# Router logits of a fused attention and mixture-of-experts kernel as half-precision products of high and low parts

## Chip, cores and metric

One Trainium2 chip, one core. The metric is the device time of one execution in microseconds (us); shown times are medians of several executions of the same program.

## What is computed

Two blocks with residuals over 4096 rows of 256 numbers. In the first, every row has its own small attention: the row is cut into 16 heads of 16, and heads attend to heads of the same row.

```python
x = x + xattn(layernorm(x), ctx, ctx)         # per row: 16x16 scores, causal, softmax, times values
xf = layernorm(x).reshape(-1, 256)
logits = xf @ gate_w.T + gate_b               # 8 experts
top1 = argmax(logits)                         # one expert a row
for e in range(8):
    y = relu(xf @ w1[e].T + b1[e]) @ w2[e].T + b2[e]
    out = out + where(top1 == e, y, 0)
x = x + out
```

The kernel takes the logits of the rows before the layer norm: they are `rstd * (x1 @ gate_w.T) + shift * sum(gate_w) + gate_b`, so the product with `gate_w` needs only x1, the outputs of the first block.

## The kernel before

Names in capitals are engines: TensorE (PE), VectorE (DVE), ScalarE (ACT), GpSimd (POOL), SyncE (SP, which only starts DMAs).

**Stage one** runs over 16 chunks of 256 rows, in 4 groups of 4 chunks. Per chunk PE makes scores (`s_ps`, 96 half-precision products, L1403), DVE takes row maxima and subtracts, ACT exponentiates (L849), DVE sums and inverts (`inverse`, L1000), POOL multiplies by the inverse (`a_sb`, L1304), PE turns the weights (`at_ps`, L1420), ACT and DVE split them into a high and a low half-precision part, and PE multiplies by the values (`pv_ps`, L1433). Queries, keys and values are split in the same way: ACT writes the high part (L786, L794, L802), POOL subtracts it from the original and writes the low part (L1282, L1289, L1296). Queries and values are then copied by DMA into block diagonals (`spread`, L601), issued by SP and ACT. DVE adds the residual and leaves x1 of the chunk in `o_sb` (L1012), 128 partitions x 32 rows x 16 heads in single precision.

**Per group**, when its 4 chunks stand in `o_sb`, PE does 4 steps of turned outputs (`tr_ps`, L1445, four transposes each) and 4 steps of gates (`lg_ps`, L1459, four heads each). ACT copies each turned step into `pay` (L842), and the next step waits for that copy (`s_x1`). From `pay` DVE takes layer-norm statistics; from the logits it chooses the expert and the slot of each row, and POOL scatters the group's 1024 rows to `sorted_rows` in DRAM by 8 indirect DMAs (L1340). The first copy of the next group into `pay` waits until these have landed (`s_scatter`).

**Stage two** runs over 39 tiles of 128 rows of one expert each: up (L1506), split of the hidden values, down (L1522, L1523), result to DRAM by an indirect DMA (L1366). It starts while the last group's logits and turned outputs are still to be done; these are woven between its first matrix products.

**The order** on each engine is written out by hand: the table `TIMES` has a number for each step of each lane, and `weave` issues the steps of an engine by these numbers. Each engine runs its instructions in that order, and a wait on one holds up all that stand behind it. A gate step is

```python
for h in range(4 * n, 4 * n + 4):
    m = eng.matmul(LG, o_sb[:, :, h], gate_bd[:, h].rearrange("p b e -> p (b e)"), start=h == 0, stop=h == HEADS - 1)
```

in which `gate_bd` (L915, made once by DVE, 128x1024) holds the gate weights in diagonal blocks. The product is in single precision; the trace has two records for each.

Of the kernel before, what the change touches and what calls it, by code (L numbers as in the profile page):

```python
# [8 lines left out]
F16 = mybir.dt.float16  # L9
# [3 lines left out]
ALU = mybir.AluOpType  # L13
# [3 lines left out]
P = 128  # L17
HEADS = 16
# [5 lines left out]
G = 8  # L24
# [51 lines left out]
    },  # L76
    "ACT": {
        "weights": (
# [136 lines left out]
    },  # L215
    "POOL": {
        "constants": (85, 155, 283),
        "tables": (399,),
# [137 lines left out]
def xattn_moe_kernel(nc, x, x_t, x_r, k_t, v_t, gate_w, gate_b, w1, b1, w2, b2, out):  # L356
# [26 lines left out]
    with stack:  # L383
# [18 lines left out]
        region = sb("region", [P, E])  # L402
        gate_bd = sb("gate_bd", [P, HEADS, 8, E])
        owner = sb("owner", [P, 8])
# [31 lines left out]
        inverse = sb("inverse", [P, BLK])  # L436
        o_sb = sb("o_sb", [P, P, HD])

        pay = sb("pay", [P, G, ROW])
# [38 lines left out]
        def carve(flat, cols):  # L478
# [52 lines left out]
        s_o_t, s_x1, s_bn, s_var1, s_rstd1, s_ln1, s_logits, s_eighths, s_gate_cols, s_gate_sum, s_gate_bd = [sem(n) for n in  # L531
            ("s_o_t", "s_x1", "s_bn", "s_var1", "s_rstd1", "s_ln1", "s_logits", "s_eighths", "s_gate_cols", "s_gate_sum", "s_gate_bd")]
        s_hot, s_seen, s_ranked, s_slot, s_tail = [sem(n) for n in ("s_hot", "s_seen", "s_ranked", "s_slot", "s_tail")]
        s_plan, s_planned, s_packed, s_digit, s_lists, s_count, s_filler = [sem(n) for n in
# [77 lines left out]
        def _(eng):  # L612
# [31 lines left out]
            def load_residual():  # L644
                for i in range(NC):
                    yield
                    sp.wait_ge(s_o_t, 4 * (i // CG))
                    sp.wait_ge(s_logits, i // CG)
                    eng.dma_start(o_sb[:, i % CG * BLK:(i % CG + 1) * BLK, :], xr_v[:, i]).then_inc(s_xr[i % CG], 16)
# [127 lines left out]
        def _(eng):  # L777
# [57 lines left out]
            def turned_rows():  # L835
                for g in range(NG):
                    for n in range(4):
# [41 lines left out]
            def relus():  # L879
                for j in range(NTILES):  # L880
# [6 lines left out]

            weave(TIMES["ACT"], spread_first_queries=spread_first_queries(), spread=spread(), queries=queries(),
                  keys=keys(), values=values(), turned_rows=turned_rows(), exponentials=exponentials(),
                  weights=weights(), expert_inputs=expert_inputs(), relus=relus())  # L890

        @block.vector
        def _(eng):
            dve = Line(eng)

            def constants():
# [15 lines left out]
                yield  # L912
                dve.wait_ge(s_select, 3)
                dve.wait_ge(s_gate, 32)
                eng.tensor_tensor(gate_bd[:], gate_sb.rearrange("p (h e) -> p h e", e=E).unsqueeze(2)  # L915
                                  .to_broadcast([P, HEADS, 8, E]), owner[:].unsqueeze(1).unsqueeze(3)
                                  .to_broadcast([P, HEADS, 8, E]), ALU.mult).then_inc(s_gate_bd, 1)
                yield
# [60 lines left out]
            def softmax():  # L979
                a = a_sb[:].rearrange("p (n k) -> p n k", k=HEADS)  # L980
                for i in range(NC):
                    yield
                    dve.wait_ge(s_qk, i + 1)
                    dve.wait_ge(s_minus_max, i)
                    eng.tensor_reduce(rowmax[:], s_ps[i % 2], AX_X, ALU.max).then_inc(s_max, 1)
                    yield
                    dve.wait_ge(s_max, i + 1)
                    dve.wait_ge(s_turned, i)
                    dve.wait_ge(s_gate_bd, 1)
# [43 lines left out]
            def choose():  # L1033
# [3 lines left out]
                for g in range(NG):  # L1037
# [9 lines left out]
                    dve.wait_ge(s_logits, g + 1)  # L1047
                    eng.tensor_tensor(v[0], lg, pay[:, :, D + 1:D + 2].to_broadcast([P, G, E]), ALU.mult).then_inc(s_hot, 1)
                    yield
# [188 lines left out]
        def _(eng):  # L1238
# [60 lines left out]
            def weights_of_softmax():  # L1299
                a = a_sb[:].rearrange("p (n k) -> p n k", k=HEADS)  # L1300
                for i in range(NC):
# [3 lines left out]
                                      ALU.mult).then_inc(s_a, 1)  # L1305

            def tables():
                yield
# [52 lines left out]
            def stores():  # L1361
                for j in range(NTILES):
# [9 lines left out]
            weave(TIMES["POOL"], constants=constants(), zeros=zeros(), statistics=statistics(), queries=queries(), keys=keys(),  # L1372
                  values=values(), weights_of_softmax=weights_of_softmax(), tables=tables(),
                  layer_norms=layer_norms(), row_tails=row_tails(), scatters=scatters(),
                  skipped_rows=skipped_rows(), residuals=residuals(), stores=stores())

        @block.tensor
        def _(eng):
# [69 lines left out]
            def gates():  # L1448
                for g in range(NG):
                    for n in range(4):  # L1450
                        yield
                        if n == 0:
                            pe.wait_ge(s_gate_bd, 1)
                            pe.wait_ge(s_o, CG * (g + 1))
                            pe.wait_ge(s_slot, 4 * g - 3)
                            if g > STAGES[0][2]:
                                pe.wait_ge(s_plan, PLAN * (g - STAGES[0][2] - 1) + 1)
                        for h in range(4 * n, 4 * n + 4):
                            m = eng.matmul(LG, o_sb[:, :, h], gate_bd[:, h].rearrange("p b e -> p (b e)"), start=h == 0,  # L1459
                                           stop=h == HEADS - 1)  # L1460
                    m.then_inc(s_logits, 1)
# [99 lines left out]
```

## Time and profile before

| | |
|---|---|
| median of 3 executions | 464.17 us (463.13 to 464.6) |
| profiled execution | span 462.9 us from its first to its last instruction; the page has no other time of it |
| busy | PE 83%, DVE 73%, ACT 39%, POOL 45% |
| chain that ended last | PE 58%, DVE 12%, issue 8%, SP's queue 7%, POOL 6%, DMA 5%, ACT 2% |

Stage one ends about 230 us into the span, stage two fills the rest. The chain follows the work that ended last back to what released it, step by step; an engine's share in it is what a faster engine could give at most. Idle times in the timeline stand in brackets behind an instruction, with what ended them.

### The profile page before, as it was taken

The page shows a single profiled execution, that of the slowest core. Times are in us where ns is not written, and L with a number is a line of the kernel's source. Part 1 is how long each engine was busy: PE and PEld are TensorE (multiplying, and loading weights), DVE is VectorE, ACT ScalarE, POOL GpSimd, SP SyncE. Part 2 cuts the span into 40 slices and gives each one's busy share as a digit, 9 for nine tenths or more (in the row PEclk, how much of TensorE's full clock was granted, in tenths as well). Part 3 has the DMA queues.
Part 4 walks back from the last instruction along what each step waited for, and adds up shares of the span by engine and source line. Part 5 has one row for each costly group of instructions (what it writes and reads, how often), then busy time and mean ns, then how long its engine had stood idle before and what let it go on. Part 6 is the DMA issues. An engine that isn't in the chain of part 4 may idle for free.

```text
span 462.9 us, 16301 instructions
## 1 busy us (share of the span) xinstructions
PE 384.6 (83%) x5889; PEld 328.5 (71%) x5889; DVE 339.8 (73%) x777; ACT 181.1 (39%) x317; POOL 207.6 (45%) x213
## 2 busy tenths in 40 slices
PE   0126878996798969895699999898999999999991
PEld 0026767996698869894688877676788888787870
DVE  8789799789882875378676987596867677766761
ACT  2344446454542523143353433243443434434320
POOL 8536444635673548643342354743333233233321
PEclk9999999955555555565589999999999999999998
DMA  7999989889778675667552544757543443434310
GB/s 264 417 254 236 264 220 260 260 188 240 200 161 218 159 160 112 180 141 219 125 143 67 107 98 106 186 139 184 106 94 99 95 108 90 104 84 106 100 29 0
DMA packets 125802, 73.17 MB, mean 158 GB/s; under 512 B 99229, under 2 KB 110238, under 8 KB 125216
## 3 DMA queue, kind: packets, MB, share of 16 engines
q1 hardware_dynamic: 96336, 60.46, 50.6%
q0 software_dynamic: 3408, 8.46, 5.0%
q10 hardware_dynamic: 25984, 3.21, 4.9%
q8 instruction: 52, 0.85, 0.7%
q14 instruction: 22, 0.18, 0.1%
HBM read 48.28 MB, written 11.24 MB: 129 GB/s over the span
## 4 chain that ended last, share of the span: by engine, by line
PE 58%; DVE 12%; issue 8%; SPq 7%; POOL 6%; DMA 5%; ACT 2%; POOLq 0%; DVEq 0%; ACTq 0%
PE s_ps L1506 19%; PE at_ps L1522 7%; PE pv_ps L1522 6%; PE s_ps L1403 6%; PE pv_ps L1433 5%; PE lg_ps L1459 4%; DMA arena<-qv_hl 3%; PE at_ps L1523 3%; PE pv_ps L1523 3%; SPq L601 3%; PE tr_ps L1445 2%; DVE arena L1186 2%; PE at_ps L1420 2%; POOL sorted_rows L1340 1%; POOL qv_hl L1296 1%
## 5 line engine op out<-in xcount | busy, mean ns | idle before, releaser
L1506 PEld LDWEIGHTS s_ps<-arena 128*128 x1872 | 131.9, 99 | 43.4 <-issue 4.9
L1506 PE MATMUL s_ps<-arena 128*128 128x128 f16 x1872 | 157.0, 221 | 2.8 <-issue 1.2
L1203 DVE SCALAR_TENSOR_TENSOR arena<-arena,s_ps 128x512 f32<-128x512 f32 x78 | 53.5, 685 | 32.5 <-PE s_ps L1506 21.1
L1433 PE MATMUL pv_ps<-a_hl,arena 128*128 128x16 f16 x1536 | 54.6, 180 | 17.1 <-DMA arena<-qv_hl 12.3
L1433 PEld LDWEIGHTS pv_ps<-a_hl,arena 128*128 128x128 f16 x1536 | 53.3, 118 | 20.7 <-DMA arena<-qv_hl 16.7
L1366 POOL DMA_INDIRECT result<-arena x39 | 38.9, 996 | 64.4 <-DVE arena L1228 60.3
L1403 PEld LDWEIGHTS s_ps<-k_hl,arena 128*128 128x128 f16 x1536 | 54.5, 118 | 15.4 <-DMA arena<-qv_hl 10.6
L1522 PE MATMUL at_ps<-arena,k_in 128*128 x160 | 60.3, 379 | 2.8 <-DVE k_hl L1214 2.8
L1359 POOL TENSOR_TENSOR arena<-arena 128x256 f32<-128x256 f32 x39 | 29.5, 756 | 73.4 <-DMA arena<-b 73.3
L1403 PE MATMUL s_ps<-k_hl,arena 128*128 128x16 f16 x1536 | 54.2, 180 | 9.7 <-DMA arena<-qv_hl 9.7
L1522 PE MATMUL pv_ps<-arena,x_in 128*128 x152 | 57.6, 379 | 0.0
L886 ACT ACTIVATE k_in<-arena 128x512 f16<-128x512 f32 x40 | 25.2, 629 | 60.5 <-DVE arena L1203 49.2
L1186 DVE SCALAR_TENSOR_TENSOR arena<-arena 128x512 f16<-128x512 f32 x56 | 47.7, 871 | 1.1 <-ACT arena L863 1.1
L863 ACT ACTIVATE arena<-arena 128x512 f16<-128x512 f32 x56 | 33.5, 623 | 33.3 <-issue 12.1
L886 ACT ACTIVATE x_in<-arena 128x512 f16<-128x512 f32 x38 | 23.9, 630 | 56.5 <-DVE arena L1203 42.0
L1523 PE MATMUL at_ps<-arena,k_hl 128*128 x160 | 43.6, 272 | 0.3 <-issue 0.3
L1523 PE MATMUL pv_ps<-arena,x_in 128*128 x152 | 41.4, 272 | 0.0
L1340 POOL DMA_INDIRECT sorted_rows<-pay,slot_i x32 | 33.2, 1037 | 15.2 <-issue 7.7
L1214 DVE SCALAR_TENSOR_TENSOR k_hl<-arena,k_in 128x512 f16<-128x512 f32 x40 | 27.4, 686 | 13.4 <-ACT k_in L886 13.0
L1282 POOL TENSOR_TENSOR qv_hl<-x_in,qv_hl 128x512 f16<-128x512 f32 x16 | 22.1, 1383 | 33.6 <-ACT qv_hl L786 33.6
L1214 DVE SCALAR_TENSOR_TENSOR x_in<-arena,x_in 128x512 f16<-128x512 f32 x38 | 27.0, 710 | 10.2 <-ACT x_in L886 9.4
L1459 PE MATMUL lg_ps<-gate_bd,o_sb 128*128 128x64 f32 x128 | 29.8, 408 | 2.3 <-DVE o_sb L1012 2.3
(141 smaller groups left out, 589.9 us busy)
## 6 DMA issues: line engine op xcount, KB each, us to landing
arena<-w SPq DMA_DIRECT2D x28, 512.0 KB, 5.1
arena<-sorted_rows SPq DMA_DIRECT2D x39, 130.0 KB, 2.2
arena<-b SPq DMA_DIRECT2D x39, 128.0 KB
arena<-qv_hl SPq DMA_DIRECT2D x70, 64.0 KB
k_in<-k_t SPq DMA_DIRECT2D x16, 256.0 KB
arena<-x SPq DMA_DIRECT2D x4, 1024.0 KB, 10.6
x_in<-x_t SPq DMA_DIRECT2D x16, 256.0 KB, 5.0
v_in<-v_t SPq DMA_DIRECT2D x16, 256.0 KB
```

Source lines behind the costliest of these rows:

```text
L886: eng.activation(h_hi[j % 2][:, c * HALF:(c + 1) * HALF], h_in[:, c], ACT.Relu).then_inc(s_h_hi, 1)
L1186: eng.scalar_tensor_tensor(out=lo, in0=src, scalar=W_SCALE, in1=hi, op0=ALU.mult, op1=ALU.subtract).then_inc(s_w_lo, 1)
L1203: eng.scalar_tensor_tensor(out=h_in[:, c].rearrange("p (k t) -> p k t", t=P), in0=bias, scalar=W_SCALE, in1=h_ps[c][:].rearrange("p (k t) ...
L1214: eng.scalar_tensor_tensor(out=h_lo[j % 2][:, cols], in0=h_in[:, c], scalar=0.0, in1=h_hi[j % 2][:, cols], op0=ALU.max, op1=ALU.subtract). ...
L1340: eng.indirect_dma_start(out=sorted_rows, out_offset=bass.IndirectOffsetOnAxis(ap=slot_i[:, b:b + 1], axis=0), in_=pay[:, b, :], in_offset ...
L1366: eng.indirect_dma_start(out=out, out_offset=bass.IndirectOffsetOnAxis(ap=rows[:, r, :].bitcast(I32)[:, D + 2:D + 3], axis=0), in_=rows[:, ...
L1403: m = eng.matmul(s[:, n], q_bd[i % 2][:, n // 2, :, n % 2, q], k_hl[:, n, k, :], start=False, stop=(n, q) == (BLK - 1, 1))
L1433: m = eng.matmul(o[:, n], v_bd[i][:, n // 2, :, n % 2, v], a_hl[:, n, a, :], start=(n, a, v) == (0, 0, 0), stop=(n, v) == (BLK - 1, 1))
L1459: m = eng.matmul(LG, o_sb[:, :, h], gate_bd[:, h].rearrange("p b e -> p (b e)"), start=h == 0, stop=h == HEADS - 1)
L1506: k = eng.matmul(o, weights_of(j, w + k_ * H + n * P, P), xt[:, j % XB, a + k_], start=(k_, w, a) == (0, HI_1, 0), stop=k_ == KD - 1 and w ...
L1522: eng.matmul(y[:], h_hi[j % 2][:, n * P:(n + 1) * P], weights_of(j, at, 2 * D), start=n == 0, stop=False)
L1523: k = eng.matmul(y[:, 0:D], h_lo[j % 2][:, n * P:(n + 1) * P], weights_of(j, at, D), start=False, stop=n == KH - 1)
```

## The change

1. DVE no longer makes `gate_bd`. It makes `gate_hl`, the gate weights times 64 in a high and a low half-precision part (two instructions of 128x128), and POOL makes the block diagonals of both parts (two instructions of 128x1024, lane `gate_blocks`).
2. For each of the 16 chunks ACT writes the high part of the chunk of `o_sb` into `o_hl`, and POOL the low part (lanes `output_halves`). `o_hl` is laid out partition, head, row, part: the elements that one of these instructions writes one after the other lie 512 bytes apart.
3. A gate step is 12 half-precision products of 128x64 in place of 4 in single precision: high by high, high by low, low by high, for each head. It waits for the high and low parts of all 4 chunks (`s_o_hi`, `s_o_lo`), where it waited for `s_o`.
4. DVE divides by 64 in the instruction that multiplies the logits by `rstd`.
5. SP's reload of `o_sb` waits for the split of the chunk that stood there, in place of the logits of its group. ACT's split of a group's first chunk waits for the logits of the group before.
6. The buffer in SBUF for descriptors of POOL's DMAs is set to 2048 bytes a partition; it had its default size.

All other numbers of `TIMES` stay.

```diff
+        "output_halves": (5316, 6999, 7544, 7821, 10139, 11102, 11887, 12396, 14641, ...    # ACT
+        "gate_blocks": (2900,),                                                            # POOL
+        "output_halves": (5386, 7069, 7614, 7891, 10209, 11172, 11957, 12466, 14711, ...   # POOL
-        gate_bd = sb("gate_bd", [P, HEADS, 8, E])
+        gate_bd = sb("gate_bd", [P, HEADS, 2, 8, E], F16)
+        gate_hl = sb("gate_hl", [P, 2, HEADS * E], F16)
+        o_hl = sb("o_hl", [P, HEADS, P, 2], F16)
...
                     sp.wait_ge(s_o_t, 4 * (i // CG))
-                    sp.wait_ge(s_logits, i // CG)
+                    sp.wait_ge(s_o_hi, i - CG + 1)
+                    sp.wait_ge(s_o_lo, i - CG + 1)
...
+            def output_halves():                                                           # ACT
+                for i in range(NC):
+                    at = slice(i % CG * BLK, (i % CG + 1) * BLK)
+                    yield
+                    act.wait_ge(s_o, i + 1)
+                    act.wait_ge(s_logits, i // CG)
+                    eng.copy(o_hl[:, :, at, 0].rearrange("p h t -> p t h"), o_sb[:, at, :]).then_inc(s_o_hi, 1)
...
-                eng.tensor_tensor(gate_bd[:], gate_sb.rearrange(...), owner[:]..., ALU.mult).then_inc(s_gate_bd, 1)
+                eng.tensor_scalar(gate_hl[:, 0], gate_sb, W_SCALE, None, ALU.mult).then_inc(s_gate_hl, 1)
+                dve.wait_ge(s_gate_hl, 1)
+                eng.scalar_tensor_tensor(out=gate_hl[:, 1], in0=gate_sb, scalar=W_SCALE, in1=gate_hl[:, 0], op0=ALU.mult,
+                                         op1=ALU.subtract).then_inc(s_gate_hl, 1)
...
+            def gate_blocks():                                                             # POOL
+                yield
+                pool.wait_ge(s_select, 3)
+                pool.wait_ge(s_gate_hl, 2)
+                for n in range(2):
+                    eng.tensor_tensor(gate_bd[:, :, n], gate_hl[:, n]..., owner[:]..., ALU.mult).then_inc(s_gate_bd, 1)
+
+            def output_halves():                                                           # POOL
+                for i in range(NC):
+                    at = slice(i % CG * BLK, (i % CG + 1) * BLK)
+                    hi, lo = [o_hl[:, :, at, n].rearrange("p h t -> p t h") for n in range(2)]
+                    yield
+                    pool.wait_ge(s_o_hi, i + 1)
+                    eng.tensor_tensor(lo, o_sb[:, at, :], hi, ALU.subtract).then_inc(s_o_lo, 1)
...
-                            pe.wait_ge(s_gate_bd, 1)
-                            pe.wait_ge(s_o, CG * (g + 1))
+                            pe.wait_ge(s_gate_bd, 2)
+                            pe.wait_ge(s_o_hi, CG * (g + 1))
+                            pe.wait_ge(s_o_lo, CG * (g + 1))
...
                         for h in range(4 * n, 4 * n + 4):
-                            m = eng.matmul(LG, o_sb[:, :, h], gate_bd[:, h]..., start=h == 0, stop=h == HEADS - 1)
+                            for a, w in ((0, 0), (0, 1), (1, 0)):
+                                m = eng.matmul(LG, o_hl[:, h, :, a], gate_bd[:, h, w]..., ...)
...
-    nc = bacc.Bacc("TRN2", target_bir_lowering=False, num_devices=1)
+    nc = bacc.Bacc("TRN2", target_bir_lowering=False, num_devices=1, dynamic_dma_scratch_size=2048)
```

Where the new instructions stand on POOL is seen in its order. In the changed kernel L1322 is the multiplication by the inverse, L1300, L1307 and L1314 are the low parts of queries, keys and values, L1375 is a scatter, L1340 the new low part of the outputs; before they were L1304, L1282, L1289, L1296 and L1340.

**POOL, around the scatters of the first group** (the chunks whose outputs are split here are those of the second group). Before:

```order
L1296 TENSOR_TENSOR qv_hl<-v_in,qv_hl 128x512
L1304 TENSOR_TENSOR a_sb<-a_sb,inverse 128x512
L1282 TENSOR_TENSOR qv_hl<-x_in,qv_hl 128x512
L1340 DMA sorted_rows<-pay,slot_i 35840x260 x3
L1289 TENSOR_TENSOR k_hl<-k_in,k_hl 128x32x16
L1340 DMA sorted_rows<-pay,slot_i 35840x260
L1296 TENSOR_TENSOR qv_hl<-v_in,qv_hl 128x512
L1304 TENSOR_TENSOR a_sb<-a_sb,inverse 128x512
L1282 TENSOR_TENSOR qv_hl<-x_in,qv_hl 128x512
L1340 DMA sorted_rows<-pay,slot_i 35840x260 x4
```

Now:

```order
L1314 TENSOR_TENSOR qv_hl<-v_in,qv_hl 128x512 [waits s_v_hi]
L1340 TENSOR_TENSOR o_hl<-o_sb,o_hl 128x32x16 [waits s_o_hi]
L1322 TENSOR_TENSOR a_sb<-a_sb,inverse 128x512 [waits s_inverse]
L1300 TENSOR_TENSOR qv_hl<-x_in,qv_hl 128x512 [waits s_q_hi]
L1375 DMA sorted_rows<-pay,slot_i 35840x260 [waits s_ln1,s_x1,s_tail,s_slot]
L1375 DMA sorted_rows<-pay,slot_i 35840x260 x2
L1307 TENSOR_TENSOR k_hl<-k_in,k_hl 128x32x16 [waits s_k_hi]
L1375 DMA sorted_rows<-pay,slot_i 35840x260
L1340 TENSOR_TENSOR o_hl<-o_sb,o_hl 128x32x16 [waits s_o_hi]
L1314 TENSOR_TENSOR qv_hl<-v_in,qv_hl 128x512 [waits s_v_hi]
L1322 TENSOR_TENSOR a_sb<-a_sb,inverse 128x512 [waits s_inverse]
L1300 TENSOR_TENSOR qv_hl<-x_in,qv_hl 128x512 [waits s_q_hi]
```

One low part stands ahead of the multiplication by the inverse, one between the fourth and the last four scatters, and a third follows the last row shown, ahead of these four.

**POOL, at the scatters of the second group.** Before:

```order
L1304 TENSOR_TENSOR a_sb<-a_sb,inverse 128x512
L1340 DMA sorted_rows<-pay,slot_i 35840x260
L1282 TENSOR_TENSOR qv_hl<-x_in,qv_hl 128x512
L1340 DMA sorted_rows<-pay,slot_i 35840x260 x3
L1289 TENSOR_TENSOR k_hl<-k_in,k_hl 128x32x16
```

Now:

```order
L1322 TENSOR_TENSOR a_sb<-a_sb,inverse 128x512 [waits s_inverse]
L1375 DMA sorted_rows<-pay,slot_i 35840x260
L1340 TENSOR_TENSOR o_hl<-o_sb,o_hl 128x32x16 [waits s_o_hi]
L1300 TENSOR_TENSOR qv_hl<-x_in,qv_hl 128x512 [waits s_q_hi]
L1340 TENSOR_TENSOR o_hl<-o_sb,o_hl 128x32x16 [waits s_o_hi]
L1375 DMA sorted_rows<-pay,slot_i 35840x260 x3
L1307 TENSOR_TENSOR k_hl<-k_in,k_hl 128x32x16 [waits s_k_hi]
```

Two low parts stand ahead of the last six scatters; the second of them is what the third group's first gate step waits for.

**POOL, at the scatters of the third group**, where stage two begins. Before:

```order
L1304 TENSOR_TENSOR a_sb<-a_sb,inverse 128x512
L1340 DMA sorted_rows<-pay,slot_i 35840x260 x6
L1359 TENSOR_TENSOR arena<-arena 128x256
L1340 DMA sorted_rows<-pay,slot_i 35840x260 x2
L1359 TENSOR_TENSOR arena<-arena 128x256 x2
```

Now:

```order
L1375 DMA sorted_rows<-pay,slot_i 35840x260
L1340 TENSOR_TENSOR o_hl<-o_sb,o_hl 128x32x16 [waits s_o_hi]
L1375 DMA sorted_rows<-pay,slot_i 35840x260
L1340 TENSOR_TENSOR o_hl<-o_sb,o_hl 128x32x16 [waits s_o_hi]
L1375 DMA sorted_rows<-pay,slot_i 35840x260 x3
L1394 TENSOR_TENSOR arena<-arena 128x256 [waits s_b2_0,s_xn2]
L1375 DMA sorted_rows<-pay,slot_i 35840x260 x2
```

Here too two low parts stand ahead of six of the eight scatters, and the last group's gates wait for the second.

## Rows read from the trace of the kernel before

**Rows 1.** The page: the span, and the chain that ended last by line.

```profile
span 462.9 us, 16301 instructions
...
PE s_ps L1506 19%; PE at_ps L1522 7%; PE pv_ps L1522 6%; PE s_ps L1403 6%; PE pv_ps L1433 5%; PE lg_ps L1459 4%; DMA arena<-qv_hl 3%; PE at_ps L1523 3%; PE pv_ps L1523 3%; SPq L601 3%; PE tr_ps L1445 2%; DVE arena L1186 2%; PE at_ps L1420 2%; POOL sorted_rows L1340 1%; POOL qv_hl L1296 1%
```

**Rows 2.** The chain in order of time: start, duration, what.

```profile
82.40 1.61 PE lg_ps L1459 x8
...
138.29 4.58 DMA sorted_rows<-pay,slot_i
142.97 0.59 ACT pay L842
143.61 1.12 PE tr_ps L1445 x4
```

**Rows 3.** Groups by shape: busy, mean ns, idle before; one row of ACT's timeline.

```profile
L1282 POOL TENSOR_TENSOR qv_hl<-x_in,qv_hl 128x512 f16<-128x512 f32 x16 | 22.1, 1383 | 33.6 <-ACT qv_hl L786 33.6
L1289 POOL TENSOR_TENSOR k_hl<-k_in,k_hl 128x512 f16<-128x512 f32 x16 | 20.1, 1255 | 10.9 <-ACT k_hl L794 10.8
...
116.69 0.79 ACT L786 CAST qv_hl<-x_in 128x512 f16<-128x512 f32 x1 [0.56 <-DVE x_in L977]
```

**Rows 4.** Timeline of PE, half-precision products: start, duration, instruction, count.

```profile
108.14 3.36 PE L1403 MATMUL s_ps<-k_hl,arena 128*128 128x16 f16 x96
111.39 0.39 PE L1468 MATMUL lg_ps<-onehot,ones_bf 128*128 128x56 bf16 x7
```

**Rows 5.** Timeline of POOL and PE, end of the first group's gates.

```profile
91.52 1.06 POOL L1304 TENSOR_TENSOR a_sb<-a_sb,inverse 128x512 f32<-128x512 f32 x1 [1.41 <-DVE inverse L1000]
...
93.49 1.06 PE L1420 MATMUL at_ps<-ident,a_sb 128*128 128x128 f32 x4
```

**Rows 6.** Timeline of POOL, second group.

```profile
119.05 1.06 POOL L1304 TENSOR_TENSOR a_sb<-a_sb,inverse 128x512 f32<-128x512 f32 x1 [3.71 <-DVE inverse L1000]
120.07 1.79 POOL L1282 TENSOR_TENSOR qv_hl<-x_in,qv_hl 128x512 f16<-128x512 f32 x1
...
132.70 1.28 POOL L1282 TENSOR_TENSOR qv_hl<-x_in,qv_hl 128x512 f16<-128x512 f32 x1 [1.80 <-ACT qv_hl L786]
...
167.61 1.06 POOL L1304 TENSOR_TENSOR a_sb<-a_sb,inverse 128x512 f32<-128x512 f32 x1 [1.34 <-DVE inverse L1000]
```

**Rows 7.** Timeline of POOL, PE and ACT, third group.

```profile
181.23 1.01 POOL L1340 DMA_INDIRECT sorted_rows<-pay,slot_i  x1 [0.17 <-issue]
...
181.78 1.97 PE L1459 MATMUL lg_ps<-gate_bd,o_sb 128*128 128x64 f32 x8
...
191.21 0.97 POOL L1340 DMA_INDIRECT sorted_rows<-pay,slot_i  x1 [0.30 <-issue]
...
196.72 0.59 ACT L842 COPY pay<-tr_ps 128x512 f32<-128x512 f32 x1 [0.49 <-issue]
...
197.53 1.09 PE L1445 MATMUL tr_ps<-ident,o_sb 128*128 128x128 f32 x4
```

**Rows 8.** Timeline of PE, POOL and ACT, last group and start of stage two.

```profile
227.91 2.00 PE L1459 MATMUL lg_ps<-gate_bd,o_sb 128*128 128x64 f32 x8 [1.71 <-DVE o_sb L1012]
...
228.54 0.97 POOL L1340 DMA_INDIRECT sorted_rows<-pay,slot_i  x1 [0.30 <-issue]
...
239.11 0.59 ACT L842 COPY pay<-tr_ps 128x512 f32<-128x512 f32 x1 [1.93 <-DMA sorted_rows<-pay,slot_i]
...
239.97 0.60 PE L1445 MATMUL tr_ps<-ident,o_sb 128*128 128x128 f32 x4
```

**Rows 9.** Timeline of DVE and POOL, the first 60 us.

```profile
20.56 1.39 DVE L915 TENSOR_TENSOR gate_bd<-a_sb,owner 128x1024 f32<-128x1024 f32 x1
...
32.04 1.27 POOL L1282 TENSOR_TENSOR qv_hl<-x_in,qv_hl 128x512 f16<-128x512 f32 x1 [4.40 <-ACT qv_hl L786]
...
52.51 0.69 DVE L1012 TENSOR_TENSOR o_sb<-pv_ps,o_sb 128x512 f32<-128x512 f32 x1
...
54.95 1.30 POOL L1296 TENSOR_TENSOR qv_hl<-v_in,qv_hl 128x512 f16<-128x512 f32 x1 [1.31 <-ACT qv_hl L802]
```

More of the change, by code:

```diff
@@ L77 @@
     "ACT": {
+        "output_halves": (5316, 6999, 7544, 7821, 10139, 11102, 11887, 12396, 14641, 15353, 16633, 16750, 19138, 19643, 20641, 20747),
         "weights": (
@@ L216 @@
     "POOL": {
+        "gate_blocks": (2900,),
+        "output_halves": (5386, 7069, 7614, 7891, 10209, 11172, 11957, 12466, 14711, 15423, 16703, 16820, 19208, 19713, 20711, 20817),
         "constants": (85, 155, 283),
@@ L532, in xattn_moe_kernel @@
             ("s_o_t", "s_x1", "s_bn", "s_var1", "s_rstd1", "s_ln1", "s_logits", "s_eighths", "s_gate_cols", "s_gate_sum", "s_gate_bd")]
+        s_gate_hl, s_o_hi, s_o_lo = [sem(n) for n in ("s_gate_hl", "s_o_hi", "s_o_lo")]
         s_hot, s_seen, s_ranked, s_slot, s_tail = [sem(n) for n in ("s_hot", "s_seen", "s_ranked", "s_slot", "s_tail")]
@@ L888, in _ @@
             weave(TIMES["ACT"], spread_first_queries=spread_first_queries(), spread=spread(), queries=queries(),
-                  keys=keys(), values=values(), turned_rows=turned_rows(), exponentials=exponentials(),
+                  keys=keys(), values=values(), turned_rows=turned_rows(), output_halves=output_halves(),
+                  exponentials=exponentials(),
                   weights=weights(), expert_inputs=expert_inputs(), relus=relus())
@@ L912, in constants @@
                 yield
-                dve.wait_ge(s_select, 3)
                 dve.wait_ge(s_gate, 32)
-                eng.tensor_tensor(gate_bd[:], gate_sb.rearrange("p (h e) -> p h e", e=E).unsqueeze(2)
-                                  .to_broadcast([P, HEADS, 8, E]), owner[:].unsqueeze(1).unsqueeze(3)
-                                  .to_broadcast([P, HEADS, 8, E]), ALU.mult).then_inc(s_gate_bd, 1)
+                eng.tensor_scalar(gate_hl[:, 0], gate_sb, W_SCALE, None, ALU.mult).then_inc(s_gate_hl, 1)
+                dve.wait_ge(s_gate_hl, 1)
+                eng.scalar_tensor_tensor(out=gate_hl[:, 1], in0=gate_sb, scalar=W_SCALE, in1=gate_hl[:, 0], op0=ALU.mult,
+                                         op1=ALU.subtract).then_inc(s_gate_hl, 1)
                 yield
@@ L988, in softmax @@
                     dve.wait_ge(s_turned, i)
-                    dve.wait_ge(s_gate_bd, 1)
+                    dve.wait_ge(s_gate_hl, 2)
                     dve.wait_ge(s_gate_cols, 1)
@@ L1047, in choose @@
                     dve.wait_ge(s_logits, g + 1)
-                    eng.tensor_tensor(v[0], lg, pay[:, :, D + 1:D + 2].to_broadcast([P, G, E]), ALU.mult).then_inc(s_hot, 1)
+                    eng.scalar_tensor_tensor(out=v[0], in0=lg, scalar=1.0 / W_SCALE,
+                                             in1=pay[:, :, D + 1:D + 2].to_broadcast([P, G, E]), op0=ALU.mult,
+                                             op1=ALU.mult).then_inc(s_hot, 1)
                     yield
@@ L1305, in weights_of_softmax @@
                                       ALU.mult).then_inc(s_a, 1)
+            def gate_blocks():
[3 more added lines that the diff above has]
+                for n in range(2):
+                    eng.tensor_tensor(gate_bd[:, :, n], gate_hl[:, n].rearrange("p (h e) -> p h e", e=E).unsqueeze(2)
+                                      .to_broadcast([P, HEADS, 8, E]), owner[:].unsqueeze(1).unsqueeze(3)
+                                      .to_broadcast([P, HEADS, 8, E]), ALU.mult).then_inc(s_gate_bd, 1)
+            def output_halves():
[5 more added lines that the diff above has]
+                    eng.tensor_tensor(lo, o_sb[:, at, :], hi, ALU.subtract).then_inc(s_o_lo, 1)
             def tables():
@@ L1373, in _ @@
                   values=values(), weights_of_softmax=weights_of_softmax(), tables=tables(),
+                  gate_blocks=gate_blocks(), output_halves=output_halves(),
                   layer_norms=layer_norms(), row_tails=row_tails(), scatters=scatters(),
@@ L1458, in gates @@
                         for h in range(4 * n, 4 * n + 4):
-                            m = eng.matmul(LG, o_sb[:, :, h], gate_bd[:, h].rearrange("p b e -> p (b e)"), start=h == 0,
-                                           stop=h == HEADS - 1)
+                            for a, w in ((0, 0), (0, 1), (1, 0)):
+                                m = eng.matmul(LG, o_hl[:, h, :, a], gate_bd[:, h, w].rearrange("p b e -> p (b e)"),
+                                               start=(h, a, w) == (0, 0, 0), stop=(h, a) == (HEADS - 1, 1))
                     m.then_inc(s_logits, 1)
```

## The prediction

> **What bounds the kernel now.** I read the page first, then the chain by line, then the chain in order of time, then the timelines of PE, POOL, ACT and DVE around the four places where logits are made, and last the groups by shape for prices. The reader should see three things. First, the gate products (L1459) are 4% of the chain of 462.9 us [rows 1], some 18 us; one step of four heads takes 1.61 us [rows 2], and there are 16 steps. So a shorter gate step can give time back, but not more than this. Second, the chain does not stay on PE in stage one. Between the first and the second group it runs through POOL: the last scatter of the first group at 138.29, its landing, ACT's copy into the same buffer at 142.97, and PE's transposes at 143.61, which had nothing else to wait for [rows 2]. What delays a scatter there delays everything. Third, POOL, though idle half of the time, is idle in stage one because it waits in order for one operand after the other; new work in its order is free only where it falls into such a wait.
>
> All sums are made against the profiled execution, span 462.9 us [rows 1]; the median of the three executions, 464.17, is 1.3 us above it, and I add the differences to the median. About 0.3% (1.4 us) is what a measurement here can tell from no change.
>
> **Prices of the new pieces.** (a) A gate step of 12 products of 128x64. The nearest rows are 96 products with 16 columns in 3.36 us, 35 ns each, and 7 with 56 down to 8 columns in 0.39 us, 56 ns each [rows 4]; the first bounds from below (0.42 us a step), 128-column weights being loaded in both; I take the second, 0.65 us, since it has nearly as many columns. So a step loses 1.0 us, and 16 steps lose 16 us of PE. (b) ACT's high part: 0.79 us, as the cast of queries at 116.69 [rows 3], which also writes 2 bytes at a time with gaps [rows 3]. (c) POOL's low part, T. The subtraction for keys, packed in runs of 16 elements, takes 1.26 us, that for queries, every second element, 1.38, and the slowest of the latter 1.79 [rows 3, 6]. The new one writes and reads each element 512 bytes from the last one, so it stands nearer to the queries; I take T = 1.38, with 1.26 and 1.79 as ends. No row here shows a step this wide.
>
> **The sum, place by place.**
>
> *First 60 us.* DVE's L915, 1.39 us [rows 9], becomes two instructions of 128x128, by size about 0.55 us together: 0.8 less on DVE, which is on the chain there. POOL gets two of 128x1024; twice L1304's 1.06 [rows 5] makes 2.1 each, 4.2 together, and POOL's idle time before 32.04 is 4.40 [rows 9]: just hidden. The first chunk's low part can start after L1012 ends at 53.20 and the cast, at 54.0, and ends at 55.4, where POOL's next step began at 54.95 [rows 9]: 0.45 late. I count half of the 0.8 as gained, since loads that must land stand behind it: together 0, ends -0.8 and +1.5.
>
> *First group.* Here the low parts fit in POOL's waits, and PE is on the chain from the first gate step past 93.49. Four shorter steps would give 4.0, but each transposes step waits for ACT's copy of the one before, and the transposes at 93.49 need POOL's 91.52 to 92.58 [rows 5], itself behind DVE work that moves by about half a microsecond; they come 1.4 earlier, the last gate step gives 1.2 more, and DVE takes 0.3 back: -2.3, ends 0 and -4.0.
>
> *Second group.* POOL now has a low part ahead of L1304 at 119.05 (its high part can come right behind ACT's cast at 116.69 [rows 3], at 117.48 to 118.27, so it ends at 119.65: 0.6 late), one ahead of the last four scatters (T), and one more right behind L1282 at 132.70 (T, and 0.1 for ACT). The 1.80 idle before 132.70 [rows 6] absorbs nothing, for it was a wait on ACT, whose cast waits for POOL's values through its DMA issues; that moves along. So the last four scatters come 0.6 + 1.38 + 1.48 = 3.5 later, and PE's transposes at 143.61 with them. The three gate steps ahead of these lie in this wait, and PE's first one waits for the last low part; only the last step, behind, gives 1.0 back: +2.5. Then a low part ahead of L1304 at 167.61 [rows 6], with 1.34 idle before it of which half is usable: +0.5.
>
> *Third group.* Low part, queries, low part stand after the scatter at 181.23, so the first gate step, which began at 181.78 [rows 7], begins at 182.2 + 1.38 + 1.28 + 1.38 = 186.3. PE makes most of this up by shorter steps. The scatters make it up nowhere: the one at 191.21 goes 2.8 later. From scatter to copy took 4.7 in the first group (138.29 to 142.97 [rows 2]), so here it was ready at 195.9 and had 0.8 to spare before 196.72. The copy comes 2.0 later, the transposes at 197.53 [rows 7] 1.8, and the gate step behind them gives 1.0 back: +0.8.
>
> *Last group.* Two low parts stand between the scatters, one on each side of that at 228.54; the first gate step moves from 227.91 to 232 [rows 8], and stage two's first products behind it, which wait later for DVE anyway and are nearly level by 239. But the copy at 239.11 waited for the scatters, without slack [rows 8]; with 2.8 more it comes at 241.9, ACT's relus stand behind it, and the transposes at 239.97 start at 242.5: +2.5. The last gate step gives 1.2 back: +1.3. After that PE is full and nothing changes.
>
> Sum: 0 - 2.3 + 2.5 + 0.5 + 0.8 + 1.3 = **+2.8, so 467.0 us**. About nine times T lies on the path: T = 1.26 makes it +1.7, T = 1.79 +6.5.
>
> DVE's changed logits instruction keeps its size, and SP's looser wait on the reload of `o_sb` moves nothing: the low part it waits for belongs to the group before, done long since. ACT's DMAs of the block diagonals come up to 1.5 us later where a cast stands ahead of them; SP's issues of the same copies end at about that time, which covers it; without that cover the second group has 0.5 more.
>
> **The rivals.**
>
> *The wide step costs POOL more.* As slow as 1.79 each, the sum is +6.5, 470.7 us. For it: no subtraction in the trace has a step over 4 bytes, and the 4-byte one is already dearer than the packed one. Against it: that rise is only 0.13 [rows 3], and the 1.79 is one instance, probably disturbed by DVE. The Trainium skill, GPSIMD Engine Reference, section Performance pitfalls for Q7 kernels, says that a step of more than 8 bytes between elements read costs about half as much again per element; no run here shows that, and by it T would be 2.07 and the time 473, an estimate.
>
> *POOL's new work is hidden and PE's gain stays.* If the scatters were not what the next group waits for, or had slack, the four places would give -2.3, -1.0, -3.0 (three steps of the third group) and -1.3: 456.6 us, faster. For it: POOL is busy under half of the time, and the chain names L1459 with four times the share of the scatters [rows 1]. Against it: the transposes at 143.61 and the copies at 239.11 start when the scatters land [rows 2, 8]. It decides at whether the low parts between the scatters cost less than the gate steps behind them give.
>
> *Gain and loss cancel.* With T at 1.26 and half of the delay of the third group taken up, within 1.4 us of 464.2.
>
> *The products are not cheaper*, because weights with a step of two elements load slowly: at 0.13 us each a step takes 1.6, the gains of 2.3, 1.0, 1.0 and 1.2 fall away, 472.5 us. Scores already load weights with gaps at 35 ns each [rows 4], so this is unlikely. The smaller descriptor buffer could make POOL wait before a scatter; with 8 scatters a group landing within 5 us each, few are open at a time.
>
> **Chances.** The forecast, 465.6 to 469.5, has 0.37; the slow wide step 0.20; the last two 0.05; cancelling 0.18; hidden 0.20. Slower by over 0.3% is 0.62, within 0.18, faster 0.20. The range reaches from part of the way to the hidden case, 459.5, to beyond the dear products with a slow T, 474.
>
> **What would show it.** Right: a group of 16 POOL subtractions for `o_hl` near 1.4 us; gate steps near 0.65; the copy that stood at 142.97 about 1 us later, that at 239.11 some 5 us later; PE waiting for POOL at the first gate step of groups two to four. Wrong: gate steps over 1 us, low parts over 1.7 us, or the copies into `pay` no later than before, which would mean that POOL's order had room.

## The result, and the profile after

The change makes the kernel slower: 491.35 us median (490.28 to 491.73) beside 464.38 for the kernel before on the same chip, a ratio of 1.0565, 95% interval 1.0513 to 1.0617. That is 27 us more by the medians, 26 by the ratio, where 2.8 were forecast, and outside the range of 459.5 to 474.0. The profiled execution has a span of 489.4 us, 26.5 above that of before [rows 1]. The mean granted clock of TensorE is 0.845 in both, so nothing here points to the clock.

The page of the changed kernel, the span and the chain that ended last by line:

```profile
span 489.4 us, 16482 instructions
...
PE s_ps L1544 18%; PE at_ps L1560 6%; PE pv_ps L1560 6%; POOL o_hl L1340 4%; POOL sorted_rows L1375 4%; PE s_ps L1439 3%; ACT o_hl L858 3%; PE at_ps L1561 3%; PE pv_ps L1561 3%; DVE arena L1204 2%; POOL a_sb L1322 2%; DMA sorted_rows<-pay,slot_i 2%; POOL qv_hl L1300 2%; PE at_ps L1456 2%; POOL qv_hl L1314 2%
```

Of the gate products, 4% of the chain before [rows 1], five steps are left in it, 3.0 us together. In their place stand the two new steps: POOL's low parts (L1340) with 4% and ACT's high parts (L858) with 3%. The scatters (L1375) went from 1% to 4%. The prices are in the groups by line and shape (busy, mean ns, idle before):

```profile
L1340 POOL TENSOR_TENSOR o_hl<-o_sb,o_hl 128x512 f16<-128x512 f32 x16 | 41.2, 2576 | 26.3 <-ACT o_hl L858 26.2
L858 ACT CAST o_hl<-o_sb 128x512 f16<-128x512 f32 x16 | 39.8, 2521 | 10.5 <-DVE o_sb L1028 10.1 <-issue 0.4
L1497 PE MATMUL lg_ps<-gate_bd,o_hl 128*128 128x64 f16 x192 | 12.1, 234 | 28.2 <-issue 24.5 <-POOL o_hl L1340 3.6
L1330 POOL TENSOR_TENSOR gate_bd<-gate_hl,owner 128x1024 f16<-128x1024 f16 x2 | 3.8, 1928 | 0.0
```

A low part takes 2.58 us where I had 1.38, a cast 2.52 where I had 0.79. How the two enter the path can be read from the chain of the changed kernel in order of time (start, duration, what), third group:

```profile
185.31 0.58 DVE o_sb L1028
185.89 0.02 issue
185.91 2.48 ACT o_hl L858
188.40 0.07 issue
188.46 2.48 POOL o_hl L1340
190.94 0.77 POOL a_sb L1322
191.71 0.05 issue
191.75 0.47 PE at_ps L1456
```

An output is ready at 185.9; five microseconds later POOL is done with its halves, and only then comes the softmax weight (L1322), which PE's next transposes wait for and which has nothing to do with the halves except its place behind them in POOL's order.

The four copies into `pay` that answer to those of before (82.43 in the first group, and 142.97, 196.72 and 239.11 [rows 2, 7, 8]), timeline of ACT after:

```profile
91.91 0.57 ACT L849 COPY pay<-tr_ps 128x512 f32<-128x512 f32 x1
...
163.19 0.58 ACT L849 COPY pay<-tr_ps 128x512 f32<-128x512 f32 x1 [3.53 <-DMA sorted_rows<-pay,slot_i]
...
223.08 0.58 ACT L849 COPY pay<-tr_ps 128x512 f32<-128x512 f32 x1 [0.28 <-issue]
...
272.64 0.58 ACT L849 COPY pay<-tr_ps 128x512 f32<-128x512 f32 x1 [3.54 <-DMA sorted_rows<-pay,slot_i]
```

They come 9.5, 20.2, 26.4 and 33.5 us late. So the loss arises in stage one, some 6 to 11 us a group, and two of the copies, the second and the last, wait for scatters, as the sum had it. Stage two gives a little back (30.7 us late at DVE's result that stood at 445.81), and the last 4.2 come back behind the last store; that is an effect of its own, below.

A low part also delays work that does not stand behind it on POOL. One of DVE's splits of the expert weights (L1204, 0.68 us otherwise) begins while the low part at 179.24 runs, and ends 0.04 us after it; DVE's low part of the turned weights (L1019), on the way to the output above, follows at once:

```profile
179.24 3.01 POOL L1340 TENSOR_TENSOR o_hl<-o_sb,o_hl 128x512 f16<-128x512 f32 x1 [0.36 <-ACT o_hl L858]
...
179.83 2.46 DVE L1204 SCALAR_TENSOR_TENSOR arena<-arena 128x512 f16<-128x512 f32 x1
182.22 0.68 DVE L1019 TENSOR_TENSOR a_hl<-at_ps,a_hl 128x512 f16<-128x512 f32 x1
```

Two more, at 87.57 and 151.81, end in the same way within 0.06 us of a low part, after 2.28 and 2.14 us. The sum had no such wait.

### The profile page after: what moved, and what is told of

Same layout as the page of the kernel before. It is cut to its first block, busy times and chain, and to the rows that moved or that the text cites. A ratio compares the mean times of both kernels' runs of the same rounds, so it can differ in the third digit from the quotient of the medians.

```text
span 489.4 us, 16482 instructions
## 1 busy us (share of the span) xinstructions
PE 366.1 (75%) x5953; PEld 310.3 (63%) x5953; DVE 353.1 (72%) x778; ACT 218.3 (45%) x333; POOL 247.0 (50%) x231
## 4 chain that ended last, share of the span: by engine, by line
PE 44%; POOL 16%; DVE 11%; issue 10%; ACT 6%; DMA 6%; SPq 4%; ACTq 1%; POOLq 0%; DVEq 0%
PE s_ps L1544 18%; PE at_ps L1560 6%; PE pv_ps L1560 6%; POOL o_hl L1340 4%; POOL sorted_rows L1375 4%; PE s_ps L1439 3%; ACT o_hl L858 3%; PE at_ps L1561 3%; PE pv_ps L1561 3%; DVE arena L1204 2%; POOL a_sb L1322 2%; DMA sorted_rows<-pay,slot_i 2%; POOL qv_hl L1300 2%; PE at_ps L1456 2%; POOL qv_hl L1314 2%
## 5 line engine op out<-in xcount | busy, mean ns | idle before, releaser
L1469 PE MATMUL pv_ps<-a_hl,arena 128*128 128x16 f16 x1536 | 53.6, 180 | 19.2 <-DVE a_hl L1019 10.4
L1204 DVE SCALAR_TENSOR_TENSOR arena<-arena 128x512 f16<-128x512 f32 x56 | 53.5, 971 | 3.4 <-ACT arena L878 3.2
L1340 POOL TENSOR_TENSOR o_hl<-o_sb,o_hl 128x512 f16<-128x512 f32 x16 | 41.2, 2576 | 26.3 <-ACT o_hl L858 26.2
L878 ACT ACTIVATE arena<-arena 128x512 f16<-128x512 f32 x56 | 34.8, 645 | 32.9 <-issue 12.5
L858 ACT CAST o_hl<-o_sb 128x512 f16<-128x512 f32 x16 | 39.8, 2521 | 10.5 <-DVE o_sb L1028 10.1
L1456 PE MATMUL at_ps<-ident,a_sb 128*128 128x128 f32 x64 | 17.6, 431 | 31.9 <-POOL a_sb L1322 31.9
L1375 POOL DMA_INDIRECT sorted_rows<-pay,slot_i x32 | 32.7, 1022 | 13.8 <-issue 7.0
L1232 DVE SCALAR_TENSOR_TENSOR k_hl<-arena,k_in 128x512 f16<-128x512 f32 x40 | 27.9, 697 | 13.8 <-ACT k_in L901 13.7
```

Source lines behind the costliest of these rows:

```text
L858: eng.copy(o_hl[:, :, at, 0].rearrange("p h t -> p t h"), o_sb[:, at, :]).then_inc(s_o_hi, 1)
L1204: eng.scalar_tensor_tensor(out=lo, in0=src, scalar=W_SCALE, in1=hi, op0=ALU.mult, op1=ALU.subtract).then_inc(s_w_lo, 1)
L1340: eng.tensor_tensor(lo, o_sb[:, at, :], hi, ALU.subtract).then_inc(s_o_lo, 1)
L1375: eng.indirect_dma_start(out=sorted_rows, out_offset=bass.IndirectOffsetOnAxis(ap=slot_i[:, b:b + 1], axis=0), in_=pay[:, b, :], in_offset ...
L1469: m = eng.matmul(o[:, n], v_bd[i][:, n // 2, :, n % 2, v], a_hl[:, n, a, :], start=(n, a, v) == (0, 0, 0), stop=(n, v) == (BLK - 1, 1))
```

## The experiments

**Is it the step between the elements?** The high and low parts get tiles of their own, laid out like the outputs, so that they are written in runs ("packed"), in three versions (both, only the high part, only the low part):

```diff
-        o_hl = sb("o_hl", [P, HEADS, P, 2], F16)
+        o_hi = sb("o_hi", [P, P, HEADS], F16)
+        o_lo = sb("o_lo", [P, P, HEADS], F16)
```

> High and low parts go into two tiles laid out like the outputs, 16 heads side by side, so that ACT and POOL write (and POOL reads) runs of 2-byte elements, and TensorE's weights take every 16th element (32 bytes apart). Theory (price: the 512-byte step makes ACT's cast 2.52 us where I had 0.79 and POOL's subtraction 2.58 where I had 1.38, and these lie on the path): cast 0.6 to 0.8, subtraction 1.1 to 1.4, gate step still about 0.8, time 460 to 469, most of the 27 us back. Rival order (the place of the new steps in the two in-order queues costs the time, whatever they last): 478 or more. Rival weights (the 32-byte step moves the cost to TensorE): gate steps of 1.5 us or more, 470 to 480.

> Only the high part is packed; the low part keeps its 512-byte step. Theory price: ACT's cast 0.6 to 0.8; POOL reads packed and writes wide, and if the write is what costs it stays near 2.5, if the read is, it falls to 1.4. Time between the two others, 468 to 480: the casts' 1.7 us each come off the path, the subtractions' 1.2 stay. Rival (only POOL counts, ACT's casts are hidden): 485 or more.

> Only the low part is packed; the high part keeps its 512-byte step, so ACT writes wide (2.5 us) and POOL reads one operand wide and writes packed. Theory price: if the write costs, the subtraction falls to 1.2 to 1.5; if the read costs, it stays over 2. Time 472 to 484. Rival (only POOL counts): as packed.

Measured, as ratios to before: packed 1.0059 (1.0025 to 1.0092), only high packed 1.0337 (1.0297 to 1.0377), only low packed 1.0355 (1.0322 to 1.0388). With 464.66 for before that is 467.4, 480.3 and 481.2 us: the second lies just above the end of its range, the other two in theirs. The groups of POOL and ACT, first of the packed version, then with only the high part packed, then with only the low part packed:

```profile
L1341 POOL TENSOR_TENSOR o_lo<-o_sb,o_hi 128x512 f16<-128x512 f32 x16 | 19.6, 1222 | 7.4 <-ACT o_hi L859 7.3
...
L859 ACT CAST o_hi<-o_sb 128x512 f16<-128x512 f32 x16 | 9.8, 615 | 9.9 <-DVE o_sb L1029 9.5 <-issue 0.4
```

```profile
L1341 POOL TENSOR_TENSOR o_lo<-o_sb,o_hi 128x512 f16<-128x512 f32 x16 | 41.4, 2615 | 10.6 <-ACT o_hi L859 10.4
```

```profile
L859 ACT CAST o_hi<-o_sb 128x512 f16<-128x512 f32 x16 | 39.9, 2524 | 10.8 <-DVE o_sb L1029 10.5 <-issue 0.2
L1341 POOL TENSOR_TENSOR o_lo<-o_sb,o_hi 128x512 f16<-128x512 f32 x16 | 25.0, 1564 | 25.8 <-ACT o_hi L859 25.7
```

The layout takes 23.5 of the 26 us away (1.0565 less 1.0059, times 464.4). On POOL the wide **write** is the dear part: it doubles the step (2.62 against 1.22), while a wide read of one operand adds 0.34. The two halves share the loss. The wide write of the low part costs 0.0278 of 464.7, 12.9 us, for 1.39 more in each of 16 steps: it counts 9.3 times, and "about nine times T" had been the forecast. How much of this goes by POOL's order and how much by DVE's waits for POOL was not measured apart. The wide high part costs 13.8 us; less 9.3 times POOL's 0.34 for reading it, 10.6 are left for ACT's 1.91 more in each, which so counts 5.5 times, an estimate. The 12.9 and the 10.6 together are the 23.5 of the layout. The rivals fall: the order alone would have kept the time at 478 or more, and ACT's casts are not hidden when they last 2.5 us. TensorE pays little for weights with 32 bytes between elements: its loads take 165 ns on average where they took 126 in the changed kernel, a gate step some 0.9 us where it took some 0.8. First the packed version, then the changed kernel:

```profile
L1498 PEld LDWEIGHTS lg_ps<-gate_bd,o_hi 128*128 128x128 f16 x128 | 13.2, 165 | 16.5 <-issue 16.2
```

```profile
L1497 PEld LDWEIGHTS lg_ps<-gate_bd,o_hl 128*128 128x128 f16 x192 | 11.2, 126 | 29.1 <-issue 28.7
```

The differences between ratios carry some 2 us of uncertainty each.

**The price by itself.** A tail behind the last row of the changed kernel, one instruction at a time with nothing beside it:

```diff
+ladder(act, eng, "wr", lambda kind, step: eng.copy(stepped(step), like(wide_in, step)) if kind == "w"
+       else eng.copy(like(narrow[:], step), stepped(step)))
```

> The changed kernel with a tail after its last row, one instruction at a time: 512 elements of 128 partitions cast or subtracted with a step of 1, 2, 4, 8, 16, 32, 64, 128 and 256 elements (2 to 512 bytes) between the half-precision elements, twice each: ACT writes and reads with the step, DVE casts and subtracts with it, POOL writes, reads, and does both. Theory price: ACT's write goes from 0.6 to 0.8 at 2 and 4 bytes to 2.5 at 512, POOL's write from 1.2 to about 2.5, a rise somewhere between; reads cost less. Rival: all steps alike here, and the 2.5 us come from other traffic in the first stage (DMA or another engine at the same time).

The busy time of ACT's write in nine stretches (two instructions in each; the steps are 2, 4, 8, 16, 32, 64, 128, 256 and 512 bytes; shown are 2, 4, 8, 16 and 512):

```profile
core 0: us, ACT busy (x), PEclk, DMA share, GB/s
487.17:488.46 1.29, 1.24 (x2) 1.00 0.00 0
488.47:490.04 1.57, 1.52 (x2) 1.00 0.02 0
490.05:492.73 2.68, 2.63 (x2) 0.67 0.00 0
492.74:497.70 4.96, 4.91 (x2) 0.50 0.00 0
...
517.31:522.29 4.98, 4.93 (x2) 0.50 0.00 0
```

POOL's write at 4, 8, 16 and 512 bytes, and its read at 4, 8, 16 and 512 bytes, in the same view:

```profile
596.06:598.47 2.41, 2.31 (x2) 0.50 0.00 0
598.53:601.28 2.75, 2.65 (x2) 0.50 0.00 0
601.33:606.35 5.02, 4.91 (x2) 0.50 0.00 0
...
626.40:631.43 5.03, 4.93 (x2) 0.50 0.00 0
```

```profile
633.94:636.56 2.62, 2.52 (x2) 0.50 0.00 0
636.62:639.27 2.65, 2.55 (x2) 0.50 0.00 0
639.33:642.46 3.13, 3.03 (x2) 0.50 0.00 0
...
655.26:658.39 3.13, 3.03 (x2) 0.50 0.00 0
```

One ACT write takes 0.62, 0.76, 1.31, 2.46 and 2.46 us: 1.7 times as much from 4 to 8 bytes, nearly twice again at 16, and then nothing more up to 512. POOL's write goes from 1.15 through 1.32 to 2.46 and stays there. Both engines write 512 elements in 2.33 to 2.47 us at any step of 16 bytes or more, and DVE's subtraction does so in 2.30 to 2.44; DVE's cast, 0.43 in runs, takes only 1.24 to 1.31 there, so the top is not the same for every instruction. Reads rise less: POOL's from 1.15 to 1.52, ACT's from 0.62 to 1.05. So neither the traffic of stage one nor the 512 bytes as such made the price; a step of 16 bytes would have cost the same. The casts and subtractions that I took prices from have no write with more than 4 bytes between elements, just below the rise.

By the Trainium skill, SBUF — State Buffer, in the note on cachelines under Door 1: The DMA port swizzle, SBUF has lines of 16 bytes, and accesses that follow each other in one line are at full rate, with at least two to a line; a step of 8 bytes still gives two. ACT's reads agree, with 0.64 us at 8 bytes and 1.09 at 16, and POOL's reads and writes nearly do, with 1.28 and 1.32 at 8 and 1.52 and 2.46 at 16; ACT's write doesn't, since at 8 bytes it already takes 1.31 where it takes 0.62 in runs, nor do DVE's (0.73 at 8 bytes for the cast).

**Late before the first output.** POOL's subtraction that stood at 32.04 [rows 9] begins at 35.40 in the changed kernel and at 35.39 in the packed one, 3.4 us late, long before there is an output to split. The timeline of DVE after:

```profile
27.84 1.88 DVE L967 SCALAR_TENSOR_TENSOR xstat<-xbn,xstat 128x8 f32<-128x8 f32 x1 [1.54 <-POOL xstat L1293]
29.65 0.41 DVE L956 BATCH_NORM_STATS2 xbn<-arena 128x6 f32<-128x256 f32 x1
29.98 2.15 DVE L1204 SCALAR_TENSOR_TENSOR arena<-arena 128x512 f16<-128x512 f32 x1
```

The 128x8 operation took 0.17 us before and the 128x512 one 0.68. While they last, POOL runs its two products for `gate_bd`, the second from 29.65 on:

```profile
27.77 3.81 POOL L1330 TENSOR_TENSOR gate_bd<-gate_hl,owner 128x1024 f16<-128x1024 f16 x2
```

The first DVE instruction ends 0.02 us after POOL's first product, the second 0.55 us after POOL's second, which is nearly its own length: 1.71 and 1.47 us more. The statistics step between them, with one input, keeps its 0.41. By the Trainium skill, Advanced Engine Details and Errata, section GPSIMD Details, POOL shares a read and a write interface with DVE and conflicts with DVE instructions that have two SBUF inputs; the trace agrees. Test: ACT makes the block diagonals, in a stretch in which it waits for DVE.

```diff
+            def gate_blocks():
+                yield
+                act.wait_ge(s_select, 3)
+                act.wait_ge(s_gate_hl, 2)
+                for b in range(8):
+                    eng.activation(gate_bd[:, :, :, b], gate_hl[:].rearrange("p n (h e) -> p h n e", e=E), ACT.Copy,
+                                   scale=owner[:, b:b + 1]).then_inc(s_gate_bd, 1)
```

> The packed version with the block-diagonal gates made by ACT, eight instructions that multiply by a column of the owner mask, at 24.7 us where ACT waits for DVE, instead of POOL's two products of 1.93 us. Theory (DVE's two-operand instructions at 27.84 and 29.98 are held up until each of these POOL instructions ends, 1.7 and 1.5 us, which is the whole 3.36 us by which everything from 31 us on is late): the rowmax at 34.45 goes back to about 31.1, the time falls by 2.5 to 4 us, to 463 to 466. Rival (the 3.4 us are slack elsewhere and are taken up by other waits): less than 1.5 us.

Measured 0.9984 (0.9956 to 1.0012), 3.5 us under the packed version. DVE and ACT now:

```profile
27.85 0.17 DVE L976 SCALAR_TENSOR_TENSOR xstat<-xbn,xstat 128x8 f32<-128x8 f32 x1 [1.54 <-POOL xstat L1302]
```

```profile
27.03 3.31 ACT L858 ACTIVATE gate_bd<-gate_hl,owner 128x256 f16<-128x256 f16 x8 [2.34 <-issue]
```

The wait is gone: POOL's subtraction begins at 32.21, 0.17 late instead of 3.36. What the wait cost lasts to the end, as far as a difference with some 2 us of uncertainty can show it.

**The descriptor buffer.** The kernel before with the one argument of the change:

```diff
-    nc = bacc.Bacc("TRN2", target_bir_lowering=False, num_devices=1)
+    nc = bacc.Bacc("TRN2", target_bir_lowering=False, num_devices=1, dynamic_dma_scratch_size=2048)
```

> The kernel before with the smaller descriptor buffer of the change and nothing else. Theory: within 0.3% of before. Rival (POOL waits for descriptors ahead of scatters or stores): 2 us slower or more.

> The kernel before with the smaller descriptor buffer alone, again, beside the two. Its trace differed at the end only: POOL's last instruction, a drain, took 2.79 us instead of 7.06. Theory: 4.3 us less at the end of every run, so 459.5 to 462.5. Rival (the first 0.55% was chance): within 1.4 us of before.

Measured 0.9945 (0.9908 to 0.9982) and again 0.9881 (0.9841 to 0.9921). What the first run was expected to do, by either theory, is missed: the kernel is faster, by 2.6 and 5.5 us. The second run's theory, 4.3 us less, holds. The last store and the span, before and with the smaller buffer:

```profile
span 462.9 us, 16301 instructions
...
455.87 0.97 POOL L1366 DMA_INDIRECT result<-arena  x1 [2.14 <-DVE arena L1228]
```

```profile
span 460.1 us, 16301 instructions
...
457.33 0.97 POOL L1366 DMA_INDIRECT result<-arena  x1 [2.13 <-DVE arena L1228]
```

From the last store's start to the end it was 7.1 us and is 2.8. In that time nothing runs but POOL's closing drain, which the trace has with 7.06 and 2.79 us. It is 2.79 in the changed kernel too, so the change got 4.3 us from it, which the sum did not have.

**What the pieces are worth without the wide step.** The shorter products alone, on the kernel before; and the packed version without low parts:

```diff
-                            m = eng.matmul(LG, o_sb[:, :, h], gate_bd[:, h].rearrange("p b e -> p (b e)"), start=h == 0,
-                                           stop=h == HEADS - 1)
+                            for n in range(3):
+                                m = eng.matmul(LG, o_top[:, :, h], gate_top[:, h], start=(h, n) == (0, 0),
+                                               stop=(h, n) == (HEADS - 1, 2))
```

```diff
-                    pool.wait_ge(s_o_hi, i + 1)
-                    eng.tensor_tensor(lo, o_sb[:, at, :], hi, ALU.subtract).then_inc(s_o_lo, 1)
+                    if i == 0:
+                        eng.memset(o_lo[:], 0.0).then_inc(s_o_lo, 1)
```

> The kernel before with the gate products alone made short: each of the 64 float32 products becomes three half-precision ones on the upper halves of the same words, nothing is split or cast and no new work stands on ACT or POOL (left out: the low halves of outputs and gates; the logits come out three times as large). Theory: this is PE's gain alone, the 2.3, 1.0, 3.0 and 1.3 us of my places without the delays on POOL, so 455 to 461. Rival (in the first stage the path is on POOL and DVE anyway, and shorter products give nothing): 463 to 465.

> The packed version without POOL's 16 low parts (the low tile is zero throughout, so the products with the low parts of the outputs add nothing), everything else kept. Theory (POOL's in-order low parts, 1.22 us each, about nine of them on the path): 6 to 11 us under the packed version, 456 to 461. Rival (low parts fit in POOL's waits): within 1.5 us of the packed version.

Measured 0.9920 (0.9885 to 0.9956) and 0.9930 (0.9905 to 0.9954), with medians of 461.23 and 462.04, both just above the ends of their theories' ranges, 461. PE's group before, then that of the first of the two:

```profile
L1459 PE MATMUL lg_ps<-gate_bd,o_sb 128*128 128x64 f32 x128 | 29.8, 408 | 2.3 <-DVE o_sb L1012 2.3
```

```profile
L1464 PE MATMUL lg_ps<-gate_bd,o_sb 128*128 128x64 bf16 x192 | 14.4, 242 | 2.3 <-DVE o_sb L1012 2.3
```

The records come to 14.4 us where those of before came to 29.8, and the kernel keeps 3.7: three quarters of what PE saves is lost even with nothing added. The low parts, at 1.22 us each, cost 6.0 us (1.0059 less 0.9930, with some 2 us of uncertainty), about five times their length and not nine: of the first 1.2 us of each more falls into waits than of the next 1.4.

**Another engine for the low parts.** Blocks on ACT, packed, all low parts on DVE, or the third and fourth of each group:

```diff
+            def output_rests():
+                for i in [k for k in range(NC) if k % CG in REST]:
+                    at = slice(i % CG * BLK, (i % CG + 1) * BLK)
+                    yield
+                    dve.wait_ge(s_o_hi, i + 1)
+                    eng.tensor_tensor(o_lo[:, at, :], o_sb[:, at, :], o_hi[:, at, :], ALU.subtract).then_inc(s_o_rest, 1)
```

> The packed version with the block-diagonal gates on ACT, and the 16 low parts moved from POOL to DVE, each one place behind its chunk's output in DVE's order. Theory (what the low parts cost is POOL's scatters and softmax weights behind them): without them and without POOL's blocks 458 would be left (462.0 less 3.5); DVE's subtraction of this size takes about 0.7 us where POOL's takes 1.22, so 458 to 462. Rival (any in-order engine of the first stage is on the path, DVE too, and waits for ACT's cast on top): 463 to 468.

> As the one before, but only the third and fourth low part of each group of chunks, those that stand among POOL's scatters, are moved to DVE; the first and second stay on POOL. Theory: most of what the low parts cost is the delay of the scatters, so this keeps most of the gain: 458 to 462. Rival (the low parts ahead of the softmax weights count as much): 462 to 465.

Measured 0.9945 (0.9918 to 0.9972) and 0.9931 (0.9887 to 0.9976), which with 465.98 for before is 463.4 and 462.8 us. Both miss the 458 to 462 of the theory and lie in the ranges of the rivals: beside the version with the blocks on ACT (0.9984) the move gives 1.8 and 2.5 us, no more than the uncertainty. Both beat the kernel before and the changed one, but both have the smaller buffer, and the kernel before with that alone stood at 0.9881 beside them. So the split products, in the best form found here, give no gain that these runs show; the lead is no larger than the buffer's alone.

## Why the prediction was wrong, step by step

- **Prices (b) and (c)** are the steps that failed. I put the new writes next to the cast and the subtraction of queries because these "write with gaps", and took 512 bytes for more of the same. The gap there is 4 bytes, and the price rises behind it, to 2.5 us for both engines. The upper end of 1.79 for T was the slowest instance of a narrow write, no bound for a wide one; for ACT I gave no end at all. The wide layout is 23.5 of the 26 us. The rival of the dearer wide step named the right mechanism on POOL, but with a price of 1.79, or 2.07 for a dear read; measured by itself, the read adds 0.37 and the write 1.31. With 2.58 for T the sum's own slope of nine would have made it +13.6, half of what came. The other half is mainly ACT's cast: the sum let it move the start of two low parts and added 0.1 for it, and it counts 5.5 times, about 10.6 us.
- **First 60 us: "just hidden"** failed by 3.4 us. I costed POOL's two block products by POOL's idle time and did not ask what DVE was doing beside them. Their size was right (1.93, forecast 2.1).
- **The smaller buffer** I looked at only for waits before scatters; it gave 4.3 us at the end.
- **PE's gain.** A gate step takes mostly 0.80 to 0.85 us (forecast 0.65) in place of 1.61 and more, so the products are cheaper as forecast. The row that I priced them by has 56 down to 8 columns, 32 on average, and not "nearly as many" as 64. I credited 2.3 + 1.0 + 1.0 + 1.2 = 5.5 us of it beside POOL's delays, and 7.6 with those hidden; without any new work on POOL the products give 3.7.
- **POOL's order** held up: the first copies of the second and last group wait for the scatters ahead of them in the changed kernel, and what the wide write adds to a low part counts 9.3 times. But that factor also holds DVE's waits for POOL, which the sum did not have, and for narrow low parts it was too high: five.
- Put together from before, in runs and traces: products -3.7, blocks on POOL +3.5, narrow low parts +6.0, buffer -4.3 make +1.5, and the packed version stands at +2.7 (1.2 to 4.3); the 1.2 between them is within the uncertainty, and ACT's narrow casts, which were not measured apart, fall into it. The layout adds 23.5. That packed comes out at the forecast 2.8 is chance: two terms that I had at nothing, +3.5 and -4.3, nearly cancel, and both the low parts (nine times 1.38 is 12.4, measured 6.0) and the gain of the products were put too high.

## What to carry to other kernels

Price a strided write by its step in bytes, not by "has gaps": measure one instruction at the step in question, or choose the layout that the elementwise engines write in runs and let TensorE read its weights with the step, which here cost some 0.1 us a gate step. A product on POOL held up a two-input instruction of DVE here for most of its own length (1.71 and 1.47 us beside 1.93), so look at DVE's timeline before calling it hidden. And where the chain runs through in-order queues of several engines, 15 us off one of them can give back little; here it was a quarter.

## What was not expected of the hardware

- Writes of 512 half-precision elements in 128 partitions take 2.46 us on ACT, 2.46 on POOL and 2.43 on DVE (its subtraction) at 16 bytes between elements and at 512; ACT's takes 0.62 in runs and 1.31 at 8 bytes. DVE's cast takes 1.30 at both.
- POOL's closing drain lasts 7.06 us with the default descriptor buffer and 2.79 with 2048 bytes: 4.3 us of a kernel's time behind its last store. How it goes with other sizes was not tried.
- A DVE instruction of 128x8 elements lasted 1.88 us, eleven times its usual 0.17, while POOL was at work on SBUF operands; with POOL's products moved to ACT it took 0.17 again.
